# Swapping the low part and the maximum in VectorE's turn of two attention loops

## What is computed

```python
h = token_encoder(x)                       # 4 layers, each: banded attention (12 heads of 16, window 64), then a feed-forward
h = h + channel_attention(layernorm(h))
h = h + one_of_4_experts(layernorm(h))
h = h + full_attention(layernorm(h))       # 12 heads of 16, all 256 keys
h = h + two_of_8_experts(layernorm(h))
```

```python
scores = q @ k.T / 4                       # banded: keys within 64 tokens only
probs  = softmax(scores)                   # needs the maximum of each row
out    = probs @ v
```

## Time and profile before

| | us |
|---|---|
| median of 3 runs | 1842.14 |
| lowest and highest | 1835.99 and 1848.72 |
| the profiled execution | 1835.38 |
| its span, first to last instruction | 1833.3 |

### The profile page before, as it was taken

The page is one execution under the profiler, slowest core; times in us unless marked ns, Lnnn a source line. Parts: engine busy times, 40 slices in busy tenths (PEclk is TensorE's granted clock), DMA queues, the critical chain, the costliest instruction groups (busy, mean ns, idle before and its releaser), DMA issues.

```text
span 1833.3 us, 39538 instructions
## 1 busy us (share of the span) xinstructions
PE 1455.2 (79%) x13098; PEld 1223.2 (67%) x13098; DVE 1242.2 (68%) x3542; ACT 979.3 (53%) x2391; POOL 815.4 (44%) x1177
## 2 busy tenths in 40 slices
PE   0589889898898887988888669759758887599992
PEld 0467678676787776777767558449636665489992
DVE  4788966889768888778896642434388997534444
ACT  0478723787435885358863123225338892155550
POOL 5576333774236862357624300125446521145540
PEclk9899999999899999999999857669969997689996
DMA  4665101643007440054600000147535421267765
GB/s 121 172 152 122 38 1 38 166 97 78 1 5 175 103 94 2 1 134 97 137 12 1 14 1 1 45 139 230 167 84 116 95 47 35 84 203 245 231 216 182
DMA packets 144278, 177.87 MB, mean 97 GB/s; under 512 B 22096, under 2 KB 106128, under 8 KB 143952
## 3 DMA queue, kind: packets, MB, share of 16 engines
q1 hardware_dynamic: 136784, 158.18, 33.6%
q0 software_dynamic: 7296, 17.18, 2.8%
HBM read 132.96 MB, written 42.34 MB: 96 GB/s over the span
## 4 chain that ended last, share of the span: by engine, by line
PE 50%; DVE 25%; issue 9%; POOL 6%; DMA 4%; ACT 3%; SPq 2%; DVEq 0%; POOLq 0%; ACTq 0%
PE bank L1474 7%; PE bank L642 7%; DVE ptl L800 7%; DVE neg_max L793 3%; PE bank L554 3%; PE bank L422 2%; PE bank L1460 2%; PE bank L440 2%; PE bank L441 2%; PE bank L442 2%; PE bank L575 2%; PE bank L443 2%; PE bank L444 2%; DVE xn L913 2%; DVE xx L767 1%
## 5 line engine op out<-in xcount | busy, mean ns | idle before, releaser
L682 ACT ACTIVATE prob<-bank,neg_max 128x192 f32<-128x192 f32 (+1 forms) x960 | 409.6, 438 | 127.3 <-DVE neg_max L793 115.3
L793 DVE TENSOR_REDUCE neg_max<-bank 128x2 f32<-128x384 f32 (+1 forms) x480 | 273.5, 571 | 84.6 <-PE bank L535 83.9
L800 DVE TENSOR_TENSOR ptl<-bank,pth 128x384 f16<-128x384 f32 (+1 forms) x480 | 275.2, 573 | 7.2 <-ACT pth L695 6.5
L554 PE MATMUL bank<-ident,prob 128*128 128x128 f32 x1536 | 267.1, 287 | 0.0
L695 ACT ACTIVATE pth<-bank 128x384 f16<-128x384 f32 (+1 forms) x480 | 245.1, 511 | 6.2 <-PE bank L554 5.7
L649 ACT ACTIVATE xx<-bank 128x256 fp32r<-128x256 f32 x256 | 95.6, 388 | 162.5 <-PE bank L422 159.1
L535 PE MATMUL bank<-kx,qx 96*128 96x192 bf16 (+1 forms) x960 | 166.7, 255 | 1.1 <-DVE xx L767 1.1
L554 PEld LDWEIGHTS bank<-ident,prob 128*128 128x128 f32 x1536 | 162.0, 142 | 0.0
L733 ACT ACTIVATE fbuf<-bank,b 128x512 f32<-128x512 f32 x96 | 66.0, 687 | 168.4 <-PE bank L444 168.4
L575 PE MATMUL bank<-v,pth 128*128 128x33 bf16 x1152 | 138.0, 179 | 21.6 <-DVE ptl L800 18.6
L642 PE MATMUL bank<-w,fbuf 128*128 128x192 f32 x768 | 140.7, 326 | 1.9 <-DVE h L890 1.9
(11 more groups left out here) (295 smaller groups left out, 4509.1 us busy)
## 6 DMA issues: line engine op xcount, KB each, us to landing
xn<-in_e_seg SPq DMA_DIRECT2D x34, 768.0 KB, 6.6
w<-in_e_w SPq DMA_DIRECT2D x23, 576.0 KB, 4.6
qk_rows<-fbuf SPq DMA_DIRECT2D x128, 96.0 KB, 2.3
qx<-qk_rows SPq DMA_DIRECT2D x35, 288.0 KB, 4.1
kx<-qk_rows SPq DMA_DIRECT2D x35, 288.0 KB, 5.8
qk_rows<-w SPq DMA_DIRECT2D x80, 96.0 KB, 2.3
qx<-qk_rows SPq DMA_DIRECT2D x35, 192.0 KB, 4.7
kx<-qk_rows SPq DMA_DIRECT2D x35, 192.0 KB, 5.5
```

The lines of the kernel that those rows point to most:

```text
L554: last = nc.tensor.transpose(bank[BT[p % 2]][:, c * P:c * P + P], probs_at(p, banded, c * P, P), ident[:, :])
L682: nc.scalar.activation(probs_at(p, banded, qt * n, n), scores_at(p, n)[:, qt, :], ACT.Exp, bias=neg_max[:, b % 2, hd, qt:qt + 1], scale=1. ...
L793: nc.vector.tensor_reduce(neg_max[:, b % 2, hd, :], scores_at(p, D if banded else S), AX.X, ALU.max, negate=True).then_inc(max_ready.sem, 1)
L800: nc.vector.tensor_tensor(ptl[:, p % 2, 0:n], bank[BT[p % 2]][:, 0:n], pth[:, p % 3, 0:n], ALU.subtract)\
```

## The change

In each turn of `dve_attention`, which serves the banded and the full attention, VectorE takes the low part of the older pair, p-4, first, and the maximum of the new pair, p, second. No instruction is added or taken away, and every wait keeps the semaphore and the value that it has. The other engines' streams are as they were.

```diff
         def dve_attention(dve, ch, it, banded, tile):
 
             for p in range(PAIRS + 8):
+                if 0 <= p - 4 < PAIRS:
+                    dve_lo(dve, it, p - 4, banded)
                 if p < PAIRS:
                     dve_max(dve, it, p, banded)
-                if 0 <= p - 4 < PAIRS:
-                    dve_lo(dve, it, p - 4, banded)
                 dve_step(dve, ch, it, p, banded, tile)
                 if banded:
                     dve_norm_step(dve, ch, it, p - 6, 0, NG - 1, 1)
```

## The result

The changed kernel takes 2068.55 us (median of 4 runs, 2063.2 to 2071.63) where the kernel before took 1839.07 in runs beside it (median of 4, 1830.68 to 1848.72): a ratio of 1.1255, 95% interval 1.1207 to 1.1302. So it is 229 us slower. The forecast was 2071, with 2048 to 2112 as its range.

The account below looks back on a forecast made before the run. No engine led before; after the change a chain from maximum through exponential, high part and low part to the next maximum would bound every turn. 1835.4 + 236 - 5 + 5 = 2071 us, range 2048 to 2112.

Parts of the forecast that it names:

- the ring: Chain maximum, exponential, high part, low part, next maximum, paid every turn: 1.90 us banded, 2.32 full attention; chance 0.80.
- The turns over the ring: Turns in 17 of 92 gaps whose VectorE steps make them exceed 1.90 us: 5.2 us per banded stage.
- The sum: Stage lengths added up: first three gaps, 92 gaps at 1.90 or 2.32 us, long turns; together +236 us.
- cover: VectorE's wait for the high part after a maximum, which hides its steps: 0.96 us banded, 1.12 full attention.
- Turn 11: Longest banded turn by VectorE's steps, with a split, a normalisation and a finish: 3.05 us.
- The tail, -5: Behind each stage's last maximum, about a maximum and a low part, 0.94 us, less; -5 us in all.
- The clock, +5: TensorE's granted clock falls in places in turns without steps, at a cost near nothing: +5 us.
- The clock rival: TensorE at 1.2 GHz bounds three quarters of four banded stages: +43 in place of +5, 2109 us; chance 0.12.
- Faster by filling VectorE's idle time: Low part runs in VectorE's 83.9 us wait for scores before the maximum: at most 1751 us; chance 0.02.
- Hidden: The swap changes under 1%, if the high part need not wait for the newest maximum: about 1840 us; chance 0.02.
- half: Alternate turns fall on projections TensorE cannot hide, so only the others lengthen: about +115, 1950 us; chance 0.04.
- The two small terms: Less work behind each stage's last maximum, -5 us, and TensorE's lower granted clock, +5 us.

## Why the prediction was right, point by point

*What led before.* The small wait was the one to read: 6.5 us for the high part became 287.3, about 310 forecast. The wait for the scores fell to 17.3, 15 forecast. ScalarE's for the maximum is 345.1, "well over twice the 115" forecast.

*The ring in every turn.* Of the 92 banded turns of a stage, 71 to 73 take 1.88 to 1.90 us, 1.90 forecast from the earlier trace rows; of those of the full attention 91 take 2.31 or 2.32, 2.32 forecast from the earlier trace rows. The runs confirm the ring from four sides: it goes when its reach becomes two turns (high part first), it grows with what stands on it (VectorE's steps, the split high part), it does not grow with what stands beside it (split exponential, doubled transposes), and the order of the two instructions without the one-turn reach does not bring it back (low part one pair older).

*The turns over the ring.* The sum put 5.2 us per banded stage on turns whose VectorE steps exceed their cover. They came, and shorter: 3.4 to 4.2 us over 1.90 in a stage. Turn 11 was taken at 3.05 us and is 2.64 in layers 2 to 4. That turn, first two rows of before, GpSimd and VectorE (the rest is the earlier trace rows), then VectorE in the changed kernel:

```profile
340.08 1.16 POOL L1064 TENSOR_TENSOR w<-qf,w 128x512 bf16<-128x512 f32 x1 [0.18 <-POOL w L1063]
...
340.65 0.75 DVE L855 SCALAR_TENSOR_TENSOR h<-hb,rstd,ln_b 128x128 f32<-128x128 f32 x1
```

```profile
382.07 0.55 DVE L793 TENSOR_REDUCE neg_max<-bank 128x2 f32<-128x384 f32 x1
...
382.99 0.35 DVE L855 SCALAR_TENSOR_TENSOR h<-hb,rstd,ln_b 128x128 f32<-128x128 f32 x1
...
384.71 0.55 DVE L793 TENSOR_REDUCE neg_max<-bank 128x2 f32<-128x384 f32 x1
```

The normalisation at L855 took 0.75 us in the turn of before and 0.35 here; that is the 0.4. An instruction's duration in one turn was carried over as if it were fixed. The trace tells what goes with the longer one: it starts while a GpSimd instruction is running (L1064, to 341.24) and ends 0.15 us after it. All 16 executions of L855 over 0.6 us before, and all 7 after, do the same, and none of the 16 shorter ones before overlaps a GpSimd instruction. In the changed kernel's turn 11, L1064 ends 0.03 us after L855 has started. That the one instruction holds up the other is read from these times; no run tried it. With this, and a ring of 1.89 rather than 1.90, the stages came to 948.2 where the sum of the prediction's five lengths is 183.8 x 3 + 184.9 + 218.7 = 955.0: 6.8 us too much.

*The tail, -5.* This step was mis-sized, and the clock took the rest. One low part fewer does stand behind the last maximum. The ends of three stages, from the last maximum to the first matmul of the output projection: the second layer before, the second layer after, the third layer after.

```profile
465.31 0.56 DVE L793 TENSOR_REDUCE neg_max<-bank 128x2 f32<-128x384 f32 x1
...
467.55 0.55 DVE L800 TENSOR_TENSOR ptl<-bank,pth 128x384 f16<-128x384 f32 x1
...
468.41 0.53 PE L554 MATMUL bank<-ident,prob 128*128 128x128 f32 x3
...
471.05 0.51 PE L450 MATMUL bank<-wb_hi,xx 128*128 128x192 f32 x1
```

```profile
544.37 0.55 DVE L793 TENSOR_REDUCE neg_max<-bank 128x2 f32<-128x384 f32 x1
...
546.02 0.54 DVE L800 TENSOR_TENSOR ptl<-bank,pth 128x384 f16<-128x384 f32 x1
...
546.95 0.88 PE L554 MATMUL bank<-ident,prob 128*128 128x128 f32 x3
...
547.87 0.49 ACT L695 ACTIVATE pth<-bank 128x384 f16<-128x384 f32 x1 [1.23 <-PE bank L554]
...
550.36 0.51 PE L450 MATMUL bank<-wb_hi,xx 128*128 128x192 f32 x1
```

```profile
826.60 0.55 DVE L793 TENSOR_REDUCE neg_max<-bank 128x2 f32<-128x384 f32 x1
...
829.11 0.53 PE L554 MATMUL bank<-ident,prob 128*128 128x128 f32 x3
...
831.80 0.51 PE L450 MATMUL bank<-wb_hi,xx 128*128 128x192 f32 x1
```

In the second layer the end takes 5.74 us before and 5.99 after; in the third 5.65 before and 5.20 after. The low part of pair 92 (the first L800 shown) starts 2.24 us behind the last maximum before the change, and 1.65 with it: 0.59 us earlier, which is one low part and not the maximum and low part, 0.94, that the step took. In the third layer the transposes still run at the full clock, 0.53 us for three, and 0.45 us of the gain is left at the end. In the second they run at the lower one: the last two sets take 0.88 each, ScalarE waits for them (1.23 us), and the 0.35 us that each set loses is more than the gain. Over the four banded stages the ends take 22.73 us after and 22.77 before. The step counted VectorE's instructions alone, where the chain behind the last maximum also runs through the transposes.

*The clock, +5.* Its fall was forecast and came. It cost nothing in the loops: in the full attention the clock was at 1.2 GHz (0.50) from 1702 to 1722 us, and the maxima there stand 2.31 or 2.32 us apart as elsewhere. The only cost of its fall seen is at the stages' ends, as above. The clock rival, 2109, fell because a TensorE turn of 1.52 us at the lower clock fits into a ring of 1.89, and doubling the transposes cost nothing. The Trainium skill ("TensorE: Matmul & The Clock Gate", section "A second HAM failure mode: psum-queue depth-cycling") tells of a kernel in which frequent short idle times between groups of matmuls make the clock go up and down between its two levels. The trace agrees: TensorE's matmuls wait 295 times for the low part, 1.3 us at most, and in the full attention the clock is 0.50 from 1600 to 1609 us, 1.00 from 1610 to 1623 and 0.50 again from 1702 to 1722.

*The other rivals.* Faster by filling VectorE's idle time (1751): the wait for the scores did shrink as that rival said, by 67 us, but the wait for the high part that took its place is 281 us longer. Hidden (1840) and half (1950) would have left stages near 143 and 163; they are 181 to 184.

*The sum.* 1835.4 + 236 - 5 + 5 = 2071 against 2068.55. The stages gave 229 instead of 236. The two small terms came to nothing together, as forecast, but smaller: what the missing low part saved at the stages' ends the clock took back there. And the base was low: 1835.4 is one execution, 3.7 us under the 1839.07 of the runs beside the changed kernel. That this nearly cancels the 7 us too much in the stages is luck; the 7 us, and not the 2.5 by which the forecast missed, are the accuracy of the sum.

## What to carry to other kernels

In a software-pipelined loop, follow the chain from an instruction through the other engines back to the same instruction, and count the turns that it spans: its length divided by that count is a floor for every turn. Swapping two neighbours on one engine's queue leaves the instructions and the data as they were, but it can take a turn from that count; here that doubled the floor, from 0.95 to 1.89 us. When a swap costs, look for the instruction of another engine that takes the span back: putting the high part ahead of the exponentials, worth nothing by itself, turned the loss of 229 us into the fastest version measured, 0.9915 of before.

## What the runs showed of the hardware beyond what was expected

- Splitting a ScalarE instruction costs little time on its chain: two copies of 128x192 back to back take 0.54 to 0.55 us, one of 128x384 0.48. For exponentials it is more: two of 128x96 take 0.57, one of 128x192 0.42.
- Redoing transposes on a TensorE that waits for others cost no time and raised its granted clock, from 0.94 to 0.99 in a banded stage and from 0.72 to 0.98 in the full attention.
- The same VectorE instruction (L855, 128x128) took 0.35 us in one turn and 0.75 in another, with the same operands' shapes. In both traces every execution over 0.6 us (16 of 32 before, 7 of 32 after) starts under a running GpSimd instruction and ends 0.15 us after it. No run tested it.
